# Cross-attention on one core: the last batch rearranged, and two elementwise steps, two activation orders and the row-maximum exchange moved in the main loop

## The reference

```
a = layer_norm(ctx, gamma, beta)
Q = x @ Wq.T ; K = a @ Wk.T ; V = a @ Wv.T         (split in 16 heads of 32)
scores = where(mask, Q K^T / sqrt(32), -inf)
out = softmax(scores) V
return x + tanh(gate) * (out @ Wo.T)
```

## Time and profile before

| what | value |
|---|---|
| time, median of 3 runs | 957.59 us (956.89 to 958.01) |
| the profiled execution's own time | 956.95 us |
| its span, first to last instruction | 955.1 us |
| mean granted TensorE clock | 0.995 |
| busy PE, DVE, ACT, POOL | 98%, 85%, 72%, 61% |

### The profile page before, as it was taken

One profiled execution on the slowest core, in us unless ns is written; L12 is line 12 of the kernel. 1 busy time (PEld: TensorE's weight loads), 2 busy tenths in 40 slices (PEclk: granted clock), 3 DMA queues, 4 the chain that ended last, 5 costly groups with the idle time before them and its releaser, 6 DMA issues.

```text
span 955.1 us, 26696 instructions
## 1 busy us (share of the span) xinstructions
PE 931.8 (98%) x10691; PEld 807.8 (85%) x10691; DVE 808.9 (85%) x1446; ACT 689.1 (72%) x1299; POOL 586.7 (61%) x665
## 2 busy tenths in 40 slices
PE   9999988999999999999999999999999999999967
PEld 8889877888888888888888888888888888888855
DVE  6962578898888889888998888899889988888896
ACT  3422677777878778877777877778787778777773
POOL 0662355666766666767666666667666667666554
PEclk9999999999999999999999999999999999999999
DMA  9983133334444333444434443334444434443101
GB/s 290 349 258 125 32 94 89 93 83 95 109 113 106 100 93 92 112 110 106 101 92 113 109 112 99 91 95 106 110 112 102 96 101 109 113 107 86 37 23 58
DMA packets 85851, 105.54 MB, mean 111 GB/s; under 512 B 22528, under 2 KB 63488, under 8 KB 85728
## 3 DMA queue, kind: packets, MB, share of 16 engines
q1 hardware_dynamic: 85152, 102.93, 41.0%
q10 hardware_dynamic: 576, 0.92, 0.3%
HBM read 86.39 MB, written 17.43 MB: 109 GB/s over the span
## 4 chain that ended last, share of the span: by engine, by line
PE 92%; DVE 5%; ACT 1%; issue 1%; POOL 0%; DVEq 0%; POOLq 0%; ACTq 0%
PE banks L932 63%; PE banks L1077 10%; PE banks L955 8%; PE banks L1090 8%; PE banks L1096 2%; DVE shared_q L838 2%; DVE rmax L828 1%; DVE banks L819 1%; ACT shared_q L603 1%; PE banks L999 0%; DVE top L816 0%; ACT shared_q L612 0%; DVE shared_r L857 0%; PE banks L963 0%; DVE shared_f L871 0%
## 5 line engine op out<-in xcount | busy, mean ns | idle before, releaser
L932 PE MATMUL banks<-shared_r,w_k 128*128 128x376 f32 x1536 | 293.1, 340 | 0.0
L932 PE MATMUL banks<-w_v,shared_r 128*125 128x512 f32 x1152 | 283.4, 395 | 0.0
L932 PEld LDWEIGHTS banks<-shared_r,w_k 128*128 128x128 f32 x1536 | 264.4, 189 | 13.0 <-issue 0.2
L475 POOL TENSOR_TENSOR shared_f<-shared_q 125x448 f32<-125x448 f32 x126 | 147.0, 1167 | 200.0 <-PE banks L1096 198.8
L828 DVE TRANSPOSE_TENSOR_REDUCE rmax<-shared_q 128x14 f32<-128x448 f32 x384 | 220.4, 620 | 57.0 <-ACT shared_q L603 56.9
L603 ACT ACTIVATE shared_q<-banks,maskT,rstd 125x448 f32<-125x448 f32 x384 | 249.6, 725 | 4.9 <-PE banks L1077 4.9
L932 PEld LDWEIGHTS banks<-w_v,shared_r 128*125 128x125 f32 x1152 | 212.5, 185 | 44.9
L838 DVE TENSOR_TENSOR shared_q<-shared_q,banks 125x448 f32<-125x448 f32 x378 | 212.0, 616 | 4.4
L612 ACT ACTIVATE shared_q<-shared_q 125x448 f32<-125x448 f32 x384 | 193.0, 569 | 6.0 <-DVE shared_q L838 5.9
L479 POOL TENSOR_TENSOR shared_f<-shared_f,shared_q 125x448 f32<-125x448 f32 x126 | 153.6, 1219 | 9.9
L455 POOL TENSOR_TENSOR shared_r<-cn,shared_r 128x375 fp32r<-128x375 f32 x124 | 112.1, 924 | 76.9 <-ACT shared_r L564 76.8
(11 more groups left out here) (94 smaller groups left out, 739.9 us busy)
## 6 DMA issues: line engine op xcount, KB each, us to landing
cn<-in_ctxT SPq DMA_DIRECT2D x128, 187.5 KB, 3.8
rows<-in_ctx SPq DMA_DIRECT2D x32, 720.0 KB
xy<-in_x SPq DMA_DIRECT2D x32, 224.0 KB, 7.4
q_kept<-shared_q SPq DMA_DIRECT2D x8, 896.0 KB, 6.9
shared_q<-q_kept SPq DMA_DIRECT2D x32, 224.0 KB, 3.9
out<-xy SPq DMA_DIRECT2D x32, 224.0 KB, 3.7
shared_f<-in_xT SPq DMA_DIRECT2D x7, 896.0 KB, 10.8
x<-row_stats SPq DMA_DIRECT2D x64, 84.0 KB
```

The source lines that it names most:

```text
L475: pool.tensor_tensor(psum[0:SP_, h, :], prob[0:SP_, q, 0, :], prob[0:SP_, q, 1, :], ALU.add).then_inc(sum_half, 1)
L932: last = pe.matmul(dst, l, m, start=(start and k == 0), stop=(stop and k == len(pairs) - 1))
```

## The change

- **Scores' banks.** Spread maxima of slot p go to bank 4 (even p) or 5 (odd p) instead of bank 0, so PE's `scores` of an even slot wait for `sub_done` only before their third chunk.
- **DVE order in a pair:** both joins of the pair before, the six quadrant maxima, both spreads, both subtractions. `top` gets a half for each parity.
- **SP:** both stores of a pair go ahead of both loads, with a semaphore for each parity.
- **ACT order in a pair:** `exponential(2m-3)` first; both `scores_out` together, `k_out(2m+2)` after them.
- **POOL** takes the multiplication of `normalise` and `low_half` from DVE.
- **The end:** the scores of slots 126 and 127 are copied out at once; the subtraction of 125 and the exponentials of 124 and 125 come behind. Slots 124 to 127 all go through `last_weighted_sums`, so POOL has no `sum_chunks` for 124 and 125. The last batch is normalised in two halves of 224 columns (a reduction over the blocks first, so the reciprocal is of 7 columns), with one high and one low copy for each half; the first low half is on POOL. `last_output` takes for each half the four products with the high part first.

```diff
@@ sync
+            def store_maxima(p):          # wait, then store of rmax, max_stored[q]
+            def load_maxima(p):
+                q = p % 2
+                sync.wait_ge(max_stored[q], p // 2 * 16 + 16)
                 if p > 1:
                     sync.wait_ge(top_done, p - 1)
...
-                exchange_maxima(2 * m)
-                exchange_maxima(2 * m + 1)
+                store_maxima(2 * m)
+                store_maxima(2 * m + 1)
+                load_maxima(2 * m)
+                load_maxima(2 * m + 1)
@@ gpsimd
+            def normalised(b):
+                pool.wait_ge(rspread_done, b + 1)
+                o = pv[:, b % 2 * HT:b % 2 * HT + HT]
+                pool.tensor_tensor(o, o, rspread[:, :], ALU.mult).then_inc(o_norm, 1)
...
+                if odd and 1 < c < B - 1:
+                    low_half(c - 2)
                 if not odd and m >= 0:
+                    if c > 1:
+                        normalised(c - 2)
...
             add_bias(B - 3)
-            sum_chunks(SLOTS - KT)
-            sum_chunks(SLOTS - KT + 1)
+            normalised(B - 2)
+            low_half(B - 2)
             result(B - 3)
             add_bias(B - 2)
             add_bias(B - 1)
+            pool.wait_ge(last_hi, 1)
+            pool.tensor_tensor(pair_of(1, 0), last_half(0), pair_of(0, 0).bitcast(F32),
+                               ALU.subtract).then_inc(last_done[0], 1)
             result(B - 2)
@@ scalar
+                if pair(m - 2):
+                    exponential(2 * m - 3)
                 if pair(m):
                     second_out(m)
...
                 if pair(m):
                     scores_out(2 * m + 1)
                 if pair(m + 1):
+                    k_out(2 * m + 2)
                     first_out(m + 1)
...
             v_out(B - 1, 2)
-            weighted_out(SLOTS - 6, 1)
-            gated_out(B - 3, KB)
+            exponential(SLOTS - 4)
+            weighted_out(SLOTS - 6)
+            gated_out(B - 3, 1)
             high_half(B - 2)
-            weighted_out(SLOTS - 4, 2)
+            exponential(SLOTS - 3)
             exponential(SLOTS - 2)
+            exponential(SLOTS - 1)
             gated_out(B - 2)
-            exponential(SLOTS - 1)
-            for k in range(KT):
-                last_high(k)
+            last_high(0)
+            last_high(1)
@@ vector
+            for m in range(PAIRS - 1):
                 slot_pair(m)
+            join_maxima(SLOTS - 4)
+            dve.wait_ge(pv_out, SLOTS - 6)
+            spread_maximum(SLOTS - 4)
+            subtract_maximum(SLOTS - 4)
+            quadrant_maxima(SLOTS - 2)
+            quadrant_maxima(SLOTS - 1)
             normalise(B - 2)
+            join_maxima(SLOTS - 3)
+            spread_maximum(SLOTS - 3)
+            subtract_maximum(SLOTS - 3)
+            join_maxima(SLOTS - 2)
+            join_maxima(SLOTS - 1)
+            spread_maximum(SLOTS - 2)
+            dve.wait_ge(sub_done, (SLOTS - 2) * ST)
+            spread_maximum(SLOTS - 1)
+            subtract_maximum(SLOTS - 2)
+            subtract_maximum(SLOTS - 1)
+            half_divide(0)
+            half_divide(1)
             last_low(1)
@@ tensor
+                    if n % 2 == 0 and j == 2:
+                        need(pe, sub_done, (n - 2) * ST)
...
             project_v(B - 1, 2)
+            pe.wait_ge(sub_done, (SLOTS - 3) * ST)
+            weighted_sums(SLOTS - 6, bank[KB])
             pe.wait_ge(s_out, SLOTS * ST)
-            weighted_sums(SLOTS - 6, bank[1])
-            pe.wait_ge(pv_out, SLOTS - 6)
-            output(B - 3, B * ST - 1, KB)
-            weighted_sums(SLOTS - 4, bank[2])
+            output(B - 3, B * ST - 1, 1)
+            pe.wait_ge(v_done, B * ST)
+            last_weighted_sums(SLOTS - 4)
+            last_weighted_sums(SLOTS - 3)
             output(B - 2, B * ST)
+            pe.wait_ge(pv_out, SLOTS - KT)
             last_weighted_sums(SLOTS - 2)
-            pe.wait_ge(pv_out, SLOTS - KT)
             last_weighted_sums(SLOTS - 1)
             last_output()
```

More of the change, by code:

```diff
@@ L138, in xattn @@
         KB, VO = 6, 7
-        spread = bank[0][:, 0:HT]
-        last_bank = {2: (bank[3], bank[4]), 3: (bank[5], bank[1])}
+        half_bank, half_den = (bank[2], bank[0]), (bank[3], bank[KB])
         sum_k, sum_v, sum_b, part = gated, xy[:, 0, :], xy[:, 1, :], gbo
@@ L202, in xattn @@
         quad_max = sem("quad_max")
-        max_stored = sem("max_stored")
+        max_stored = [sem(f"max_stored{q}") for q in range(2)]
         ld_max = [sem(f"ld_max{q}") for q in range(2)]
@@ L225, in xattn @@
         last_hi = sem("last_hi")
-        last_done = sem("last_done")
+        last_done = [sem(f"last_done{i}") for i in range(2)]
         block = es.enter_context(nc.Block())
@@ L495, in slot_pair @@
                     result(c - 3)
+                if m == PAIRS - 2:
+                    low_half(B - 3)
                 for n in (2 * m + 6, 2 * m + 7):
@@ L674, in slot_pair @@
                 c, odd = divmod(m, 2)
+                if pair(m - 2):
+                    exponential(2 * m - 3)
                 if pair(m):
                     second_out(m)
-                if odd and c > 1:
+                if odd and 1 < c < B - 1:
                     high_half(c - 2)
@@ L862, in last_divide @@
[L862 to L873, removed]
-                dve.tensor_tensor(last_chunk(k), o, d, ALU.mult).then_inc(last_norm, 1)
@@ L902, in slot_pair @@
                     normalise(c - 2)
[L903 to L905 removed]
+                if pair(m - 1):
+                    join_maxima(2 * m - 2)
+                    join_maxima(2 * m - 1)
                 quadrant_maxima(2 * m)
                 quadrant_maxima(2 * m + 1)
[L908 to L920 removed]
+                if pair(m - 1):
+                    spread_maximum(2 * m - 2)
+                    spread_maximum(2 * m - 1)
+                    subtract_maximum(2 * m - 2)
+                    subtract_maximum(2 * m - 1)
+            for m in range(PAIRS - 1):
+                slot_pair(m)
+            join_maxima(SLOTS - 4)
[4 more added lines that the diff above has]
+            quadrant_maxima(SLOTS - 1)
+            normalise(B - 2)
+            join_maxima(SLOTS - 3)
[10 more added lines that the diff above has]
+            half_divide(1)
             last_low(1)
[L922 to L925 removed]
             last_result()
@@ L1051, in last_output @@
                 pe.wait_ge(y_out, B - 2)
-                for k in range(KT):
-                    for e, (a, d) in enumerate(PASSES):
-                        if e == 0:
-                            pe.wait_ge(last_hi, k + 1)
+                for i in range(2):
+                    pe.wait_ge(last_hi, i + 1)
+                    for a, d in ((0, 0), (0, 1), (1, 0)):
                         if a == 1:
-                            pe.wait_ge(last_done, k + 1)
-                        last = pe.matmul(bank[KB][0:T, :], oT[:, a, k, :], wo[:, d, k, :],
-                                         start=(k == 0 and e == 0),
-                                         stop=(k == KT - 1 and e == len(PASSES) - 1))
+                            pe.wait_ge(last_done[i], 1)
+                        for k in (2 * i, 2 * i + 1):
+                            last = pe.matmul(bank[1][0:T, :], oT[:, a, k, :], wo[:, d, k, :],
+                                             start=(k + a + d == 0), stop=(k == KT - 1 and a == 1))
                 last.then_inc(y_mm, 1)
@@ L1112, in last_weighted_sums @@
             def last_weighted_sums(p):
-                to, to_den = last_bank[p % KT]
+                q, i = p % 2, p % KT // 2
+                at = slice(q * T, q * T + T)
                 for j in range(ST):
                     pe.wait_ge(exp_done, p * ST + j + 1)
-                    weighted(p, j, to[:, 0:T])
-                    last = denominator(prob[:, p % NB, j, :], to_den[:, 0:T], j == 0, j == ST - 1)
+                    weighted(p, j, half_bank[i][:, at])
+                    last = denominator(prob[:, p % NB, j, :], half_den[i][:, at],
+                                       j == 0, j == ST - 1)
                 last.then_inc(pv_mm, 1)
```

106 lines of the change are left out of this document (47 added, 59 removed).

## The result

The changed kernel takes 940.36 us in the median of 4 runs (939.77 to 942.75), the kernel before 957.8 in the runs beside it; the ratio is 0.9831, interval 0.9816 to 0.9847. Predicted: 941.0, range 938 to 948. The profiled execution has a span of 938.4 us; the sum in the prediction, before its allowance for the clock, was 938.1.

What follows compares the result with a forecast made beforehand. PE, busy 98% of the span, bounds the kernel; only its early and late gaps can give time. Span 955.1 - 5.8 - 11.2 = 938.1, plus 1.85 and 0.64 gives 940.6; with half the clock loss 941.0, range 938 to 948.

Steps and rivals of the forecast that it cites:

- The loop costs nothing: Main loop: PE is busy throughout at 13.09 us a pair, and the reordered work stays under cover; cost 0.
- The thin cover of the K copy: Each pair: ACT's K copy, behind six score copies, ends at T+4.32 before PE needs it at T+4.72; slack 0.4 us.
- the slower rival: K copy late in every pair, PE losing the excess in some 60 pairs; 964.6 us at 0.4 excess; chance 0.05.
- The early gaps: Pairs 1 to 6: PE's waits of 1.06, 1.56 and 1.88 us and the slow K group go; 5.8 us gained.
- SP's order costs nothing: SP's stores ahead of its loads: even load up to 0.6 us later, odd about 2 us earlier, used a pair later; cost 0.
- the prediction's own signs of being wrong: A pair growing by 0.1 us, early waits that stay, or a DVE join idle for a DMA by several us.
- The end: After the loop: the last DVE instruction starts at 940.45 instead of 951.62; 11.2 us gained.
- The load of 84 KB: In the end, the load before the join of 127: 3.0 us taken, between 2.1 and 5.9; 2.2 by the skill's formula.
- The half-size operations: Last batch's halves on DVE: reduction and spread 0.38 us each, reciprocal 0.24, product 0.39.
- The clock: PE's clock may fall between gaps at 927.7 to 930.1, holding half 1 back by 0.9 us; half of that put in.
- The rival of a held end: End held by a new wait: 5.9 us loads, full-width halves, low clock; end gains 6.4, time 945.8; chance 0.17.
- POOL: Takes a multiply and a subtraction in every second pair, 1.15 to 1.61 us bounds; covered in the loop, cost 0.

Runs made afterwards that it cites:

- k_pad_large: Changed kernel with two unused ACT copies of 448 columns in front of the K copy of each pair from 6 on; 965.6 us, ratio 1.0096.
- loop_as_before: Changed kernel with the five edits of the main loop undone for pairs up to 61, the new end kept; 945.76 us, ratio 0.9881.
- exp_behind_sums: Changed kernel with ACT's exponential of the odd slot back behind the copy of the weighted sums, pairs up to 61; 941.01 us, ratio 0.9838.
- maxima_first: Changed kernel with DVE's old order up to pair 61: six maxima, then join, spread and subtraction slot by slot; 940.92 us, ratio 0.9829.
- multiply_on_dve: Changed kernel with normalise's multiplication and the low half back on DVE for batches up to 30; 943.14 us, ratio 0.9853.
- end_tight: Changed kernel with its end reordered: DVE's joins and last maxima before 124's spread, ACT's copy of sums 122 before 124's exponential; 941.12 us, ratio 0.9837.
- wait_first_chunk: Changed kernel with PE's wait for the subtractions before a pair's first score chunk instead of the third; 940.42 us, ratio 0.9825.
- store_load_in_turn: Changed kernel with SP's old order, store, load, store, load, throughout; 946.22 us, ratio 0.9884.

## Why the prediction was right

*The loop costs nothing.* Right: 54 pairs take 706.67 us, 706.69 before. The thin cover of the K copy was the step most at risk. Its times came out to 0.02 us; k_pad_large shows that beyond the cover there is a real wait with a price of 0.47 us a pair, enough to make the kernel slower than before; and its size is some 0.47 us rather than 0.4. So the slower rival had the right place, and that cover is what kept it from coming true.

*The early gaps.* Right in size (5.55 against 5.8), with one releaser wrong: pair 6's first K waits 0.54 us, not 0.2, and for the copy of the weighted sums, not for its own K copy; K's clock did not fall, and the group took 2.31 us instead of 3.71. Undone one by one, the multiply gives 0.79 back, SP's order 2.44, the wait's place 0.55 and DVE's order 0.50; all together 5.54 (loop_as_before). ACT's exponential put back alone is 0.67 better early (exp_behind_sums). The place of its K copy was not undone by itself, and how the edits act together was not separated.

*SP's order costs nothing.* The step's reason was wrong. I wrote that both loads are used a pair later; but with the join ahead of the maxima the first load that is late holds up everything on DVE, and in the end the odd load is on the path. Keeping the old order costs 4.95 us. The sum was not hurt because the walk of the end itself used the new order and put the load on the path.

One of the prediction's own signs of being wrong did show, a join of DVE that sits idle for a load by several us. In the changed kernel it is in pair 1:

```profile
109.48 0.45 DVE L841 TENSOR_REDUCE top<-x 128x14 f32<-128x168 f32 x1 [4.09 <-DMA x<-row_stats]
111.62 0.45 DVE L841 TENSOR_REDUCE top<-x_odd 128x14 f32<-128x168 f32 x1 [1.69 <-DMA x_odd<-row_stats]
```

No cost of it is seen: PE's scores of pair 2 start at 119.32 without a wait, and in maxima_first, where DVE waits 4.97 us for scores at that place and for no load, early is 0.50 us longer. The sign was badly chosen for pair 1.

*The end.* 11.48 against 11.2 us. Last scores copied at once 6.84, halves 1.60, SP's order 2.51, multiply and low half on POOL 2.73: undone singly they make 13.7, more than the whole, so they overlap. The load of 84 KB was the one unknown: from its issue to the join it took 3.34 us (921.72 to 925.06), where 3.0 was taken; the 2.2 us that the prediction gives as an estimate is too short by over 1 us (and by the prediction's own times it would have made the sum 0.25 us better, not 0.4). DVE waited 0.65 us for it. From the load's issue to the last subtractions the prediction had 4.9 us and the trace has 4.78: the load was longer, and the join and the two spreads shorter (1.44 against 1.9), so two errors cancelled, which was luck. The half-size operations measured 0.39, 0.20, 0.41 and 0.39 us, where 0.38, 0.24, 0.38 and 0.39 stood.

*The clock.* I had put in half of 0.9 us for a fall behind PE's gap in the end. The gap was 1.35 us and the clock stayed at 1.00, so the sum without the allowance, 940.6, was the better number. The rival of a held end counts half of the fall twice, once in the 941.0 that it starts from: from 940.6 its terms (2.9, 1.0, 0.9) give 945.4, not 945.8. It did not come to pass.

*POOL.* The multiply took 1.14 to 1.16 us in the end (mean 1.156), under the 1.22 of the earlier trace rows. POOL's addition of two SBUF inputs went from a mean of 1.22 us to 1.15, and with the multiply and the low half back on DVE (multiply_on_dve) it takes 1.28:

```profile
L497 POOL TENSOR_TENSOR shared_f<-shared_f,shared_q 125x448 f32<-125x448 f32 x124 | 142.3, 1148 | 9.7
...
L497 POOL TENSOR_TENSOR shared_f<-shared_f,shared_q 125x448 f32<-125x448 f32 x124 | 158.9, 1282 | 9.7
```

(groups by line and shape, the changed kernel and then multiply_on_dve). So DVE's operations with two SBUF inputs lengthen POOL's beside them, and DVE's multiply took 1.61 us beside POOL's work. The Trainium skill, SBUF — State Buffer, section Who interferes with whom, says that a DVE instruction with two SBUF inputs contends with a GpSimd instruction that reads SBUF; the traces agree with it.

## What to carry to other kernels

When one engine is busy throughout a loop, look for its gaps at the loop's start and end, walk both from rows of the trace, and check that the loop's covers survive the reordering: here a copy 0.94 us later in each pair, with 0.47 us of cover, turned 17 us faster into 8.6 us slower. Look at the order of transfers together with the order of what uses them: with the joins ahead of the maxima, keeping SP's old order cost 2.4 us early, and 2.5 us in the end. When undoing single edits gives more than the total, and a further cut on one engine gives nothing, look for a second chain that is level with the first, as in end_tight; that shortening both would help is argued, no run here did it.

## What the runs showed of the hardware

- Where a join of DVE waited for a load of 84 KB, the join started 2.9 to 4.4 us after the load's issue (2.86 in wait_first_chunk, 4.36 in the changed kernel at 132.51). In the end of store_load_in_turn a store of 21 KB took 2.14 us from its issue to that of the load which waits for it, and 3.15 us when it was issued right behind a load (issues at 921.63, 923.77, 924.39 and 927.54).
- Of four gaps of PE, one of 1.35 us left the clock at 1.00, one of 1.88 us in pair 5 of the kernel before was followed by a fall to 0.50 and one of 1.88 us at 917 was not, and one of 6.75 us was followed by 0.50 and matmuls of 5.12 in place of 3.06 us. The windows behind the two of 1.88 us, in the kernel before:

```profile
160.40:162.00 1.60, 1.60 (x8) 1.60 (x6) 1.43 (x6) 1.52 (x3) 1.41 (x2) 0.50 0.87 236
...
920.50:922.00 1.50, 1.50 (x12) 1.22 (x7) 1.47 (x3) 0.29 (x1) 1.42 (x2) 1.00 0.27 93
```

- DVE's last low half, two SBUF inputs of 224 columns, took 0.78 us at 933.06 in the changed kernel, while POOL's addition ran from 932.30 to 933.59, and 0.39 us in end_tight, where POOL's had ended at 933.57 and it started at 933.85.
- In k_pad_large the weight loads waited 0.6 us for the K copy and the matmuls behind them only 0.19, and the pair grew by 0.47: the idle time of neither row alone is the price.
- The time before the main loop differs between executions: pair 1 starts anywhere from 100.28 to 101.93 us. It pays to compare two profiles from a common point inside the program.
